# Edge sums of a graph network on one core: 80 chunks instead of 78 share their sums, ScalarE makes one one-hot in four

## What is computed

```python
in_agg = segment_sum(edge_feat, receivers, num_segments=6250)
out_agg = segment_sum(edge_feat, senders, num_segments=6250)
h = relu(concatenate([in_agg, out_agg, node_feat], axis=1) @ W1 + b1)
x = layernorm(x + h @ W2 + b2)
```

## Time and profile before

| | us |
|---|---|
| median of 3 runs | 1354.76 (1354.26 to 1355.96) |
| the profiled execution's own time | 1358.4 |
| its span in the trace | 1356.6 |

### The profile page before, as it was taken

One profiled execution on the slowest core, in us unless ns is written; L12 is line 12 of the kernel. 1 busy time (PEld: TensorE's weight loads), 2 busy tenths in 40 slices (PEclk: granted clock), 3 DMA queues, 4 the chain that ended last, 5 costly groups with the idle time before them and its releaser, 6 DMA issues.

```text
span 1356.6 us, 60124 instructions
## 1 busy us (share of the span) xinstructions
PE 1129.9 (83%) x21795; PEld 917.9 (68%) x21795; DVE 1167.1 (86%) x3489; ACT 926.2 (68%) x2047; POOL 1084.1 (80%) x663
## 2 busy tenths in 40 slices
PE   2667588988898888898888889989888898899596
PEld 2546377877787777787777767767666676777443
DVE  6756689988999999998899989999879898999486
ACT  6233588988898888888788876666566676666242
POOL 3888888888888888888888888888888888888533
PEclk9976789999999999999899989999989998999798
DMA  9332489999998899998999998889878887888441
GB/s 300 49 43 17 62 182 209 212 195 199 203 215 203 200 202 205 209 210 199 207 235 243 241 217 210 199 209 216 212 166 209 192 200 188 185 195 207 79 133 45
DMA packets 251312, 247.53 MB, mean 182 GB/s; under 512 B 105587, under 2 KB 213460, under 8 KB 250966
## 3 DMA queue, kind: packets, MB, share of 16 engines
q1 hardware_dynamic: 158632, 216.16, 52.4%
q0 software_dynamic: 92384, 28.77, 27.8%
q10 hardware_dynamic: 144, 0.48, 0.1%
HBM read 139.12 MB, written 106.21 MB: 181 GB/s over the span
## 4 chain that ended last, share of the span: by engine, by line
POOL 33%; DMA 26%; issue 23%; PE 11%; DVE 4%; ACT 2%; SPq 1%; POOLq 0%; ACTq 0%; DVEq 0%
POOL out_tables L775 32%; DMA out_tables<-payload,target 23%; PE psum L1679 3%; DMA feat<-in_edge_attr 2%; PE psum L1890 2%; PE psum L1845 1%; PE psum L1902 1%; PE psum L1655 1%; ACT slots_out L870 1%; DMA rows_i<-in_dst 1%; PE psum L1618 1%; DVE same L1357 1%; PE psum L1628 0%; ACT parts L849 0%; ACT payload L887 0%
## 5 line engine op out<-in xcount | busy, mean ns | idle before, releaser
L775 POOL DMA_INDIRECT out_tables<-payload,target x628 | 1050.7, 1673 | 209.4 <-issue 170.0
L1679 PE MATMUL psum<-parts,to_slot 128*128 128x194 bf16 x4524 | 457.9, 251 | 88.7 <-ACT slots_out L870 75.0
L1679 PEld LDWEIGHTS psum<-parts,to_slot 128*128 128x128 bf16 x4524 | 377.9, 99 | 136.1 <-ACT slots_out L870 92.6
L870 ACT ACTIVATE slots_out<-psum 128x388 bf16<-128x388 f32 x780 | 341.7, 499 | 68.4 <-PE psum L1679 54.2
L1703 PE MATMUL psum<-to_node,slots_in 64*64 64x313 bf16 x9360 | 353.3, 301 | 24.6 <-issue 19.9
L1703 PEld LDWEIGHTS psum<-to_node,slots_in 64*64 64x64 bf16 x9360 | 278.2, 108 | 85.4 <-issue 33.4
L1291 DVE TENSOR_SCALAR to_slot<-iota_h,slot 128x480 bf16<-128x480 f16 (+1 forms) x936 | 291.3, 367 | 29.6 <-PE psum L1679 29.1
L1330 DVE TENSOR_SCALAR to_node<-iota_h,slot_rel 128x318 bf16<-128x318 f16 x780 | 239.7, 329 | 0.0
L1330 DVE TENSOR_SCALAR to_node<-iota_rows,slot_rel 128x318 bf16<-128x318 f16 x520 | 181.8, 350 | 0.0
L887 ACT ACTIVATE payload<-psum 128x256 f32<-128x256 f32 x157 | 58.9, 375 | 159.5 <-PE psum L1757 87.1
L937 ACT ACTIVATE apart<-iota_h,slot_rel 128x318 bf16<-128x318 f16 x260 | 131.9, 551 | 12.0 <-DVE slot_rel L1302 10.3
(11 more groups left out here) (138 smaller groups left out, 894.6 us busy)
## 6 DMA issues: line engine op xcount, KB each, us to landing
slot_tiles<-slots_out SPq DMA_DIRECT2D x156, 388.0 KB
feat<-in_edge_attr SPq DMA_DIRECT2D x195, 256.0 KB
slots_in<-slot_tiles SPq DMA_DIRECT2D x152, 242.5 KB
slots_in<-slot_tiles SPq DMA_DIRECT2D x152, 230.4 KB
slot_tiles<-slots_out SPq DMA_DIRECT2D x78, 194.0 KB
out_tables<-payload,target POOLq DMA_INDIRECT x628
out_tables<-zeros POOLq DMA_DIRECT2D x4, 1600.0 KB
feat<-out_tables SPq DMA_DIRECT2D x48, 128.0 KB, 2.3
```

Of the source, the lines that this page charges most:

```text
L775: e.indirect_dma_start(out_tab, at, payload[b][:, t, :], None, element_offset=k * TABLE_ROWS * D, compute_op=ALU.add).then_inc(s_tab[k], 16)
L870: e.activation(slots_out[b][:, g:g + n, m, :], round_bank(b, r)[:, 0:n * SLOT_W].rearrange("p (g w) -> p g w", w=SLOT_W), ACT.Copy).then_i ...
L1679: last = e.matmul(round_bank(b, r)[:, o:o + SLOT_W], to_slot[m][:, COLUMN_FROM[k] + t * P:COLUMN_FROM[k] + (t + 1) * P], parts[b][:, SHARE ...
```

## The change

- `SUMS` 14 instead of 16: 14 chunks go whole at the end and 80 share. There are now 160 tiles for each pair of groups, 1,600 in all. Unit 0 takes 20, unit 13 takes 160, and the 12 between take 118.3 each.
- `ROUND` 4 instead of 6: ScalarE makes every fourth one-hot, VectorE three of four.
- `RING` 6 and `PARTS` 10: parts of 16 tiles, a ring of 6 buffers, and the first ring's worth fetched during the last 12 pairs of sharing chunks.
- In the summing units the addresses of the first quad's columns are written right after the windows, those of the others where all were before.
- `in_group` is made in six subtractions, one for each of 6 columns, with a wait behind each.

```diff
-SUMS = 16
+SUMS = 14
-RING = 4
-PARTS = 2 * RING
+RING = 6
+PARTS = 10
-ROUND = 6
+ROUND = 4
...
         def targets_apart(c):
-            return isinstance(c, int) and c in (0, END_SHARE)
+            return isinstance(c, int) and (c == 0 or END_SHARE <= c < N_CHUNKS)
...
+        def ring_buf(g, p):
+            return (g * PARTS + p) % RING
...
             def ranks(n):
                 e.wait_ge(s_from_group, n + 1)
-                step(e.tensor_tensor(in_group[:, :, :, :], from_group[:, :, 0:SLOT_GROUPS, :], from_group[:, :, 1:, :],
-                                     ALU.subtract))
+                for k in range(MINI):
+                    last = e.tensor_tensor(in_group[:, k, :, :], from_group[:, k, 0:SLOT_GROUPS, :], from_group[:, k, 1:, :],
+                                           ALU.subtract)
+                    if k < MINI - 1:
+                        last.then_inc(s_in_group, 1)
+                        e.wait_ge(s_in_group, (MINI - 1) * n + k + 1)
+                step(last)
...
             def relative(g, p):
-                e.wait_ge(s_slot_in[p % RING], 16 * LOADS * (g * (PARTS // RING) + p // RING + PIECES))
+                e.wait_ge(s_slot_in[ring_buf(g, p)], 16 * LOADS * ((g * PARTS + p) // RING + PIECES))
...
                     if q == 1:
                         for h in range(HALVES):
                             add_window(c, b, ats, h)
+                        targets(c, b, c, mode, (0, QUAD))
                     if q == QUADS - 1:
...
-                        targets(c, b, c, mode)
+                        targets(c, b, c, mode, (QUAD, mode.cols))
```

More of the change, by code:

```diff
@@ L326, in build @@
         s_from_group = sem("s_from_group")
+        s_in_group = sem("s_in_group")
         s_masked = sem("s_masked")
@@ L445, in targets_no @@
                 return c + 1 + (1 if c > 0 else 0)
-            return c + (2 if mode is SHARING else 3)
+            if mode is SHARING:
+                return c + 2
+            return c + 2 + (c - END_SHARE if mode.sums else SUMS)
         def quad_buf(q, b, mode):
@@ L627, in load_tiles @@
                     e.dma_start(into[j:P:LOADS, :], homes[both * g:both * (g + 1), 2 * j:2 * j + 2, a * SLOT_W:z * SLOT_W]
[L628 removed]
+                                ).then_inc(s_slot_in[ring_buf(g, p)], 16)
                 at = HOME_AT[MINI] + shared * g
                 e.dma_start(into[LOADS - 1:P:LOADS, :], slot_rows[at:at + shared, a * SLOT_W:z * SLOT_W]
[L631 removed]
+                            ).then_inc(s_slot_in[ring_buf(g, p)], 16)
             def load_part(g, p):
@@ L936, in to_far @@
                 k = i - PART_FROM[p]
-                e.activation(apart[:, n % APARTS, :], iota_h[:, 0:HOT], ACT.Abs, bias=slot_rel[p % RING][:, k:k + 1],
+                e.activation(apart[:, n % APARTS, :], iota_h[:, 0:HOT], ACT.Abs, bias=slot_rel[ring_buf(g, p)][:, k:k + 1],
                              scale=-1.0).then_inc(s_apart, 1)
@@ L1329, in tiles_to_nodes @@
                         hot, numbers = hot.rearrange("p (a k) -> p a k", k=HOT // HOT_ROW), iota_rows[:, :, 0:HOT_ROW]
-                    e.tensor_scalar(hot, numbers, slot_rel[p % RING][:, k:k + 1], None, ALU.is_equal).then_inc(s_to_node, 1)
+                    e.tensor_scalar(hot, numbers, slot_rel[ring_buf(g, p)][:, k:k + 1], None, ALU.is_equal).then_inc(s_to_node, 1)
             def targets(c, b, d, mode, columns=None):
@@ L1703, in product @@
                     return e.matmul(ps_groups[g % 2][h][cols, 0:GROUP_NODES],
-                                    slots_in[p % RING][rows, j - PART_FROM[p], D * k:D * (k + 1)],
+                                    slots_in[ring_buf(g, p)][rows, j - PART_FROM[p], D * k:D * (k + 1)],
                                     to_node[rows, node_buf(g, j), 0:GROUP_NODES], start=(j == 0 and k < 2), stop=(j >= TILES - 2 and k == 2))
```

8 lines of the change are left out of this document (3 added, 5 removed).

## The result

The changed kernel takes 1339.49 us (median of 4 runs, 1334.06 to 1342.05), the kernel before 1355.36 beside it: ratio 0.9876, 95% interval 0.9845 to 0.9907. It is faster by some 16 us, where I had forecast 35. The time lies near the upper end of my range (1305 to 1341). The profiled execution is the fastest of the four, 24.3 us under the profiled one of before.

The account below looks back on a forecast made before the run. It took POOL's scatters as the bound before the change. Two more sharing chunks (+16.2), early tests (-2.5) and the summing stage (-48.8) made -35.1 us: 1323.3 by the profiled execution, 1319.8 forecast, range 1305 to 1341.

Parts of the forecast that it names:

- 32.2 us for a middle unit: Summing stage: each of the 12 middle units takes 32.2 us, bounds 30.6 and 36.
- 0.9 over: Middle units: time beyond the fullest engine's work is 0.9 us a unit, where it was 1.3 before.
- start of unit 0: Before the summing stage: two more sharing chunks cost +16.2 us, the early tests give -2.5.
- early tests: One-piece subtraction split into short pieces lets POOL's scatters in between: -2.5 us, between -7.6 and +1.5.
- to the first matmul on the sums: After the last tile: 6 us to that matmul, where late last scatters made it 19.5.
- the ring: Slot parts in the summing stage: a ring of six takes 0.9 us a unit off VectorE's waits for parts.
- TensorE's 31.3: Middle units: TensorE is the fullest engine, needing 31.3 us a unit after 27.1 before.
- A, POOL the bound: Summing stage: POOL still sets the time, 32 fewer scatters count in full, -47.4 us, 1307.4 us; chance 20%.
- B, slower scatters: Summing stage: scatters slow to 2.03 us beside more plain one-hots, -21.0 us, 1333.8 us; chance 10%.
- C, `to_node` as dear as `apart`: ScalarE in middle units: a tile costs 0.91 us, its unit 33.0, +20 us, 1340 us; chance 10%.
- D, ScalarE's waits stay: Middle units: ScalarE's 5.3 us of waits a unit remain, unit 35.4, some 1358 us, slower than before; chance 12%.
- The first quad's addresses: Summing units: writing them early gains nothing by itself, only covers the case that POOL catches up.

Follow-up runs that it names:

- dma_light: Changed kernel with only the first half of each slot part's tiles fetched in the summing stage, first kind of chip: 1319.16 us, ratio 0.9709 to the kernel before.
- dma_light2: The edit of dma_light repeated on the changed kernel, on another chip of the first kind: 1319.87 us, ratio 0.9724 to the kernel before.
- pe_short: Changed kernel with each tile matmul covering half of the columns, same number of instructions, first kind of chip: 1334.57 us, ratio 0.9846 to the kernel before.
- again2: The changed kernel unaltered, run again on a chip of the first kind: 1342.72 us, ratio 0.9891 to the kernel before.
- again3: The changed kernel unaltered, run once more on another chip of the first kind: 1342.82 us, ratio 0.9899 to the kernel before.
- sums16b: Changed kernel with 78 sharing chunks and 16 whole ones, as before the change, first kind of chip: 1353.64 us, ratio 0.997 to the kernel before.
- act_light: Changed kernel with ScalarE's one-hots a third as wide, second kind of chip: 1423.59 us, ratio 1.0363 to the kernel before.

## Why the prediction was right and wrong

The direction was right: POOL is no longer the bound, and two units fewer bring more than two sharing chunks cost. The step that failed is the 32.2 us for a middle unit, with its "0.9 over" the fullest engine. Against the profiled execution, by my own terms:

| term | forecast | measured | difference |
|---|---|---|---|
| start of unit 0 (sharing chunks, early tests) | +13.7 | 807.00 - 790.92 = +16.1 | +2.4 |
| unit 0 | 11.7 | 11.8 | +0.1 |
| 12 middle units | 386.4 | 393.5 | +7.1 |
| last unit | 42 | 44.2 | +2.2 |
| to the first matmul on the sums | 6 | 6.2 | +0.2 |
| tail after it | same | 69.5 for 70.8 | -1.3 |
| sum | -35.1 | -24.3 | +10.8 |

The work of each engine in a unit was right within 1.1 us. What was wrong is the time over the fullest. I had read 1.3 over in the kernel before, put it down to mutual waits, and expected the ring to take a part of it off. It is 2.3 (32.8 less TensorE's 30.5), and 16.9/12 = 1.4 of this are the stops before blocks of instructions. dma_light and dma_light2 show that they come from the load on the DMAs: with two fifths less traffic (128 to 130 GB/s for 214), nearly all are gone, and a unit is 31.3 and 31.5, which is 1.3 to 1.6 us less. That alone is more than the 0.6 a unit that I missed. pe_short shows that the stop fills the time which faster matmuls leave. That the stops are a wait for instructions is read from their count and from the times of the packets, and no run changed the supply of instructions alone; that the load of the transfers makes them, and that they carry the missing time, is shown.

Two of my errors partly cancelled. TensorE's 31.3 was 0.8 too high. And the 0.9 was too low even without the stops: in dma_light and dma_light2 TensorE is busy 29.8 and 29.9 us a unit, and the units are 1.5 and 1.6 longer. So part of the nearness of 32.2 to 32.8 is luck.

The kernel before showed the stops too, had I asked what TensorE's tile matmuls wait for from 820 to 1225 us:

```profile
PE psum L1703 <- issue: 17.5, 21, 1.6
```

I had taken 0.212 a tile from 12 tiles without a stop among them.

The rest is which execution I compared. I was 19.7 us below the measured median: 10.8 of them are in the table, 5.4 are that the profiled execution of the changed kernel (1334.06) is its fastest, and 3.6 are what I took off because the profiled one of before lay above its median. (1323.3 less 3.6 is 1319.7 and not the prediction's 1319.8.) The median of the kernel before was 1355.4, 1356.7 and 1358.1 in the three sets, so little had to come off. Between medians the gain is 16, 14 and 15 us. In the profiled execution of again2, 17.5 us longer than that of the result, unit 0 starts at 823.34 and not 807.00, so that 16.3 of the 17.5 lie ahead of the summing stage. The +2.4 there is of the same kind: a sharing chunk is (807.00 - 166.10)/80 = 8.01 us and was (790.92 - 168.22)/78 = 7.98, and 0.03 by 80 makes 2.4. In again3 it is (812.11 - 165.82)/80 = 8.08. So the length of a sharing chunk varies from execution to execution by as much as what remains to be explained, and I can't settle it.

Rival by rival:

- A, POOL the bound: no. POOL issues its last scatter at 1241.09 us, 15 us before the last tiles at 1256.5, and waits 11.8 us for addresses. But it is near, as sums16b shows.
- B, slower scatters: no. (332.1 + 75.9)/207 = 1.97 us with these waits, 1.91 without.
- C, `to_node` as dear as `apart`: no. ScalarE needs 30.2 us a unit, forecast 30.1.
- D, ScalarE's waits stay: half. They are 31.5 us in 12 units, 2.6 each and not 5.3, nearly all for TensorE. act_light shows that ScalarE's load hardly matters even where the kernel loses.

"Slower than before" happened on another chip, by a mechanism that was no rival of mine: TensorE stops more often, and so issues 42.5 instructions per us against 49.8, in a change that makes it the fullest engine. The parts: 80 and 14 chunks carry 11 us on the first kind and lose some 32 on the second. The early tests gave nothing that shows, where I had forecast 2.5 us. The first quad's addresses gave nothing that shows, as forecast. The ring's 11 us stay untested on the first kind.

None of the kernels with the full computation beats the changed one on the first kind, or the one before on the second.

## What to carry over

When a change takes an engine from 90% to 93% busy, read its own idle rows first: time that waits for nothing ("issue") does not shrink with the other engines' waits, and a rate taken from a dozen instructions leaves it out. In long unrolled stretches of short instructions, count them per us, look whether stops recur after the same number, and whether they end a fixed time after an instruction packet. A time in one trace is not yet a gain: the 2.1 us of the early tests were there in a second trace of the kernel before. And a version that is balanced to within 3% on one chip may lose on the next, so leave room on the engine that differs.

## What the runs showed of the hardware

- On chips of the first kind TensorE stops for 0.3 to 1.4 us, often after 123 pairs of matmul and weight load, where its code is unrolled and the DMA engines are 0.89 busy; 26 of 27 stops end 2.0 to 2.9 us after an instruction packet of 16.4 KB started. At 0.68 it hardly stops (1 and 5 stops for 27 and 31). There was one such packet per 4.9 and 5.0 us whether 123 matmuls took 4.4 us or 2.6.
- Two matmuls of 64x128 on the two row halves start 3 ns apart, and the next two 140 ns later. Between them and ones of 64x64, the step is 224 and 250 ns. Mixed so, a pair of tiles takes 0.64 us in place of 0.43 for the same product.
- The same program ran at 49.8, 49.1 and 49.7 TensorE instructions per us in three sets of runs and at 42.5 on another chip, all at a granted clock of 0.99 or 1.00, and the mean step within a run of tile matmuls was 33 ns on both kinds. On the second kind the kernel before lost 1 to 3%, the changed one 7%.
